# GpSimd takes 1536 of the 4096 columns in every round of an expert ranking's comparisons

## The reference

```python
logits = tokens @ router_w.T
probs = jax.nn.softmax(logits, axis=-1)
top1_idx = jnp.argmax(probs, axis=-1)
top1_prob = jnp.max(probs, axis=-1)
order = jnp.lexsort((-top1_prob, top1_idx))     # by expert, then most certain first, then by index
...
keep_sorted = pos_in_group < capacity           # ceil(4096 / 8 * 1.25) = 640
keep = jnp.zeros((T,), bool).at[order].set(keep_sorted)
return jnp.where(keep, top1_idx, 0).astype(jnp.int32)
```

## Time and profile before

| | |
|---|---|
| runs | 5526.91, 5540.9 and 5541.35 us, median 5540.9 |
| profiled execution | span 5525.2 us from the first to the last instruction; its own device time is not recorded apart from that |
| busy over the span | TensorE 4705.2 us (85%), VectorE 3719.1 (67%), ScalarE 2827.0 (51%), GpSimd 2810.2 (51%) |
| the 32 rounds | 3904.6 to 4002.9 us, 98.3 us or 1.8% of the span |

### The profile page before, as it was taken

The page is one execution under the profiler, slowest core; times in us unless marked ns, Lnnn a source line. Parts: engine busy times, 40 slices in busy tenths (PEclk is TensorE's granted clock), DMA queues, the critical chain, the costliest instruction groups (busy, mean ns, idle before and its releaser), DMA issues. The chain is left out here.

```text
span 5525.2 us, 143465 instructions
## 1 busy us (share of the span) xinstructions
PE 4705.2 (85%) x57069; PEld 3341.4 (60%) x57103; DVE 3719.1 (67%) x8589; ACT 2827.0 (51%) x6227; POOL 2810.2 (51%) x3349
## 2 busy tenths in 40 slices
PE   7699999999999999999999999954375999945886
PEld 3366666666666666666666666633263666623665
DVE  7677777777777777777777677748724656667442
ACT  2266565666666656666666656631022666641332
POOL 4477666777677667766777667601022333311000
PEclk9899999999999999999999999977587999967897
DMA  0211111111111111111111110000211000010002
GB/s 21 70 29 25 25 34 35 25 25 34 36 25 25 31 31 29 25 34 31 28 24 34 25 24 20 17 24 2 67 50 32 2 2 1 1 24 13 26 29 56
DMA packets 312162, 150.60 MB, mean 27 GB/s; under 512 B 146143, under 2 KB 301003, under 8 KB 311243
## 3 DMA queue, kind: packets, MB, share of 16 engines
q1 hardware_dynamic: 309451, 137.20, 10.3%
q0 software_dynamic: 2048, 4.20, 0.3%
HBM read 101.10 MB, written 27.41 MB: 23 GB/s over the span
## 5 line engine op out<-in xcount | busy, mean ns | idle before, releaser
L1435 POOL TENSOR_TENSOR loc_a<-loc_a,loc_b 128x512 f32<-128x512 f32 x768 | 976.9, 1274 | 234.0 <-DVE loc_b L1511 233.5
L1123 PE MATMUL psum<-loc_wqk,loc_xt 128*128 128x512 f32 x1536 | 828.9, 622 | 15.3 <-issue 4.7
L1186 PE MATMUL psum<-loc_m,xn_rows 128*128 128x128 f32 x6144 | 823.7, 277 | 4.8 <-DVE y_rows L1543 3.0
L1307 ACT ACTIVATE loc_sq<-psum 128x512 f32<-128x512 f32 x768 | 455.1, 593 | 682.6 <-PE psum L1123 681.3
L1460 POOL TENSOR_TENSOR loc_a<-loc_a,loc_rn 128x512 f32<-128x512 f32 x768 | 785.4, 1045 | 0.1
L1186 PEld LDWEIGHTS psum<-loc_m,xn_rows 128*128 128x128 f32 x6144 | 754.3, 193 | 48.2 <-issue 45.5
L1507 DVE TENSOR_TENSOR loc_a<-psum,loc_rope 128x512 f32<-128x512 f32 x768 | 523.2, 681 | 332.4 <-ACT loc_sq L1307 318.3
L1467 POOL TENSOR_TENSOR xn_cols<-xn_cols,loc_rec 128x512 f32<-128x512 f32 x384 | 394.1, 1047 | 685.3 <-DVE loc_rec L1538 684.9
L1344 ACT COPY xn_rows<-psum 128x512 f32<-128x512 f32 x768 | 411.7, 588 | 219.6 <-PE psum L1174 215.9
L1511 DVE TENSOR_TENSOR loc_b<-psum,loc_rope 128x512 f32<-128x512 f32 x768 | 520.5, 678 | 0.0
L1515 DVE TENSOR_REDUCE loc_n<-loc_sq 128x8 f32<-128x512 f32 x768 | 516.9, 673 | 0.0
(11 more groups left out here) (372 smaller groups left out, 8565.0 us busy)
## 6 DMA issues: line engine op xcount, KB each, us to landing
loc_x<-loc_shifted SPq DMA_DIRECT2D x192, 256.0 KB, 4.0
loc_shifted<-y_rows SPq DMA_DIRECT2D x144, 64.0 KB
loc_wqk<-in_L_ffn_Wqkv SPq DMA_DIRECT2D x24, 256.0 KB, 3.7
x_rows<-y_rows SPq DMA_DIRECT2D x96, 64.0 KB
x_rows<-y_rows SPq DMA_DIRECT2D x96, 63.5 KB
moe_w<-in_L_ffn_W SPq DMA_DIRECT2D x16, 256.0 KB, 4.7
l3a_qk<-l3a_rot SPq DMA_DIRECT2D x16, 256.0 KB, 2.1
grp_w<-in_L_ffn_W SPq DMA_DIRECT2D x16, 256.0 KB, 4.2
```

The source lines that it names most:

```text
L1123: nc.tensor.matmul(ring("p", i, unit), xt[:, b % 2, t * P:(t + 1) * P], wqk[:, unit * 512:(unit + 1) * 512], start=True, stop=True).then_i ...
L1186: last = nc.tensor.matmul(y_bank[:, 0:P], u[:, i % 2, h // 2, h % 2, :], m[:, h, :], start=(h == 0), stop=(h == HEADS - 1))
L1307: nc.scalar.activation(sq[:, g % 2, :], ring("p", i, unit), ACT.Square).then_inc(sem["squared"], 1)
L1435: nc.gpsimd.tensor_tensor(part, part, b_[:, g % 2, :], ALU.add).then_inc(sem["added"], 1)
```

## The change

In each round the 1536 columns that lie farthest from the diagonal block are compared by GpSimd: the last 1536 in rounds 0 to 15, the first 1536 in rounds 16 to 31. VectorE compares the other 2560, with as many instructions as before. TensorE waits in each round for both, VectorE's `compared` and the new `far_compared`. GpSimd waits, like VectorE, for `counted` before it writes a half of `above` again.

```diff
             names = ("turned", "router_ready", "logits_done", "exp_ready", "shifted", "top_ready", "top_stored", "top_spread",
-                     "onehot_ready", "compared", "counted", "blank_ready", "dve_step")
+                     "onehot_ready", "compared", "far_compared", "counted", "blank_ready", "dve_step")
...
+            FAR = 12 * P
+            early = lambda j: j < NT // 2
...
                         pe.wait_ge(sem["compared"], j + 1)
+                        pe.wait_ge(sem["far_compared"], j + 1)
...
                     nc.gpsimd.memset(core.y[:, :, :], 0.0).then_inc(sem["blank_ready"], 1)
+                    pool.wait_ge(sem["top_ready"], 1)
+                    pool.wait_ge(sem["top_spread"], 16)
+                    for j in range(NT):
+                        if j >= 2:
+                            pool.wait_ge(sem["counted"], j - 1)
+                        far = slice(TOK - FAR, TOK) if early(j) else slice(0, FAR)
+                        nc.gpsimd.tensor_scalar(above[:, j % 2, far], row[:, far], top[:, j:j + 1], None,
+                                                ALU.is_le if early(j) else ALU.is_lt).then_inc(sem["far_compared"], 1)
...
-                        after(nc.vector.tensor_scalar(above[:, m, 0:d1], row[:, 0:d1], mine, None, ALU.is_lt))
+                        start, stop = (0, TOK - FAR) if early(j) else (FAR, TOK)
+                        after(nc.vector.tensor_scalar(above[:, m, start:d1], row[:, start:d1], mine, None, ALU.is_lt))
...
-                            nc.vector.tensor_scalar(above[:, m, d1:TOK], row[:, d1:TOK], mine, None, ALU.is_le)
+                            nc.vector.tensor_scalar(above[:, m, d1:stop], row[:, d1:stop], mine, None, ALU.is_le)
```

## The result

| | before | after |
|---|---|---|
| time, median of 5 runs | 5532.54 us | 5621.43 us |
| runs from, to | 5526.91, 5541.35 | 5617.63, 5631.2 |
| ratio after / before | | 1.0165, 95% interval 1.0151 to 1.0179 |
| span of the profiled execution | 5525.2 us | 5618.9 us |

A forecast was written before the change was run, and what follows sets the result against it. VectorE's four instructions were taken to bound the 32 rounds; each loses 2.53 us to GpSimd and saves 0.80, so 1.73 us longer, 55.5 us in all, span 5580.7 us, median 5590 us, range 5543 to 5640.

The forecast's parts named there:

- the forecast's own band: For the 32 rounds: a loss of 1.9 to 3.2 us a round, +35 to +77 us, given 42%.
- the raw row: Rival, 18%: GpSimd's comparison really costs 2.58 ns per column and holds VectorE throughout; round 6.19 us, +101 us, about 5636 us.
- What bounds the rounds, and that a microsecond in a round is 32 in the end: In the 32 rounds VectorE's four instructions set the 3.03 us pace; nothing hides it, so 1 us a round makes 32 us.
- What VectorE gives up, 0.80 us a round: VectorE's comparisons lose 1536 columns at 0.519 ns each; alone its round falls from 3.03 to 2.23 us, saving 25.5 us.
- That the engines exclude each other: In the rounds GpSimd and VectorE take turns, so VectorE's round becomes 2.23 us plus the time GpSimd holds it up.
- The 2.53 us of GpSimd's hold: GpSimd's 1536-column comparison at 1.65 ns per column holds VectorE up 2.53 us in each round.
- the cleaning of the 512-column row: A GpSimd row outside the rounds: 1.633 us less 0.60 of supposed waiting and 0.19 fixed leaves 0.84 us, 1.65 ns per column.
- TensorE's second wait and GpSimd's wait for `counted` at nothing: In the rounds both waits add nothing, at most the end of one round; GpSimd may be a round ahead of VectorE.
- Line rate: Rival, 22%: GpSimd compares at its memset pace, 0.83 ns per column; a round loses 1.28 us, the kernel 15.5, about 5550 us.
- Beside each other: Rival, 12%: GpSimd's comparison holds VectorE up under 0.80 us a round or not at all; at best 25.5 us less, about 5515.
- Its tell-tales: Signs in the rounds: 32 GpSimd rows of 2.5 us or more, stretched VectorE rows summing to some 150 us, matmuls every 4.8 us.

The follow-up runs named there:

- the run beside: Kernel before, VectorE still comparing all 4096 columns; GpSimd adds the same 32 comparisons of 1536 columns into a tile nobody reads or waits for: 6.54 us a round.
- the probes: Kernel before, with single GpSimd instructions (512 to 1536 columns) ahead of the rounds, each beside 24 short VectorE instructions; 768 columns stretched one-input ones twice by 0.64 us.
- the run with three instructions: Changed kernel with GpSimd's 1536 columns a round split into three instructions of 512 columns in place of one: 5.79 us a round.

## Why the prediction was right, and where not

Measured 5621 us, predicted 5590, range 5543 to 5640, slower with 0.76. It is slower, by 1.6%. The cost of the change was put at 55.5 us and is 89 us. That lies above the forecast's own band (+35 to +77 us, 42%) and below the rival of the raw row (+101): none of the stated cases names it. The time is within the range because the range reaches up to that rival, not because the forecast's sum was right.

**What bounds the rounds, and that a microsecond in a round is 32 in the end: right.** 89.7 us in the rounds of one profile, 89 us between the medians. That they agree so closely is in part luck, since the rest of the kernel wanders by more than their difference. TensorE's granted clock stayed at 0.50, as it was forecast.

**What VectorE gives up, 0.80 us a round: right.** With ScalarE as the partner 1024 columns saved what the slope says (1024 x 0.519 = 0.53 us, 3.03 to 2.50). The 1536 columns were not measured without a hold; between the run beside and the changed kernel they are worth 6.54 - 5.85 = 0.69 us. The missing 0.11 us lie in the holds: in the run beside GpSimd meets `tie`, which costs VectorE less, 22 times instead of 14.

**That the engines exclude each other: right in direction, too simple in form.** Shown by GpSimd's work beside VectorE with nobody waiting for it: 3.51 us more a round. The prediction left open whether they take turns by whole instructions or by parts of one, and reckoned with the whole. The Trainium skill's page SBUF — State Buffer, section "Who interferes with whom", says that whoever comes first has the shared ports for its whole instruction. For GpSimd's two-input instructions and for its cast (1.46 us) I have seen nothing else. For its tensor-scalar instruction the probes contradict it: up to 1024 columns VectorE stands still twice for a third of the time, and between the two it is free. Here the measurement decides.

**The 2.53 us of GpSimd's hold: the term that was mis-sized.** The step that failed is the cleaning of the 512-column row: "So GpSimd seems to have waited 0.20 + 0.40 us and to have been ahead at the end." It had not waited to speak of: 512 columns take 1572 ns with nothing beside, against the row's 1633. That VectorE's `cd_u` and `cd_base` ran undisturbed inside it fits the probes: `cd_u` falls into the part that keeps nobody out, `cd_base` has two inputs, which the last part does not keep out, and the stretched one-input `cd_gap` at 4901.76 meets that last part. This is read off the sizes of the parts; that place itself was not tried again. The raw row gave 4.15 us for the instruction (0.19 + 3.96), and 4.16 us is what it takes.

Of this VectorE loses 3.51 us in the run beside (6.54 - 3.03), where the forecast had 2.53. So the sum should have been 32 x (3.51 - 0.80) = 87 us, and 89 are measured: nearer to the rival "the raw row" (+101) than to the forecast (+55.5). In the changed kernel the loss is 3.62 us by the pace (5.85 - 2.23) and 3.6 us by the count of held rows above. It is less than the 3.96 of the rival since it depends on what GpSimd meets: the probes are held for 3.90 us with one input (4.08 - 0.18) and for 3.02 with two (3.23 - 0.21), and half of the 32 holds in the rounds fall on instructions with two inputs.

**TensorE's second wait and GpSimd's wait for `counted` at nothing: right.** TensorE waits for VectorE alone in the profile after, and a third buffer changes nothing (5.88 against 5.85 us). GpSimd does wait for `counted`, 42.2 us in all, but nobody waits for it.

**The rivals.** Line rate falls: 2.52 ns per column where 0.83 was needed. The raw row had the price of the instruction right and the hold too long; it also called GpSimd the slower engine, and that is wrong, as its 4.15 us are less than a round of 6.19 or of 5.85, and TensorE waits for VectorE. The Trainium skill's sentence on one-input work (GPSIMD Engine Reference, "4.1 Engine selection") holds here for the cast (0.83 ns per column, as the memsets) and not for a comparison. "Beside each other" falls with the probes and the run beside. It would have needed a hold of 1536 columns under 0.80 us. Fewer columns do not help either: with 512 GpSimd holds VectorE for 0.42 us at a time, but saves it only 0.27 us a round, and there GpSimd is late.

**Its tell-tales.** GpSimd's rows of over 2.5 us and the stretched small instructions were seen as said. VectorE's sum was to be some 150 us and is 184.6, and the pace of 4.8 us was 5.85.

## What to carry to other kernels

Before work goes to an idle engine, ask whether that engine can work at the same time as the one it relieves: look in the trace for one instruction of each that overlap, and compare the row's maximum with its median. What the change takes off the busy engine (here 0.80 us a round) must be more than the time for which the helper keeps that engine standing (here 3.5 us). That the helper is idle and its own time free says nothing of this. An instruction that runs undisturbed inside another engine's long row does not show that the other one was waiting: it may have been in a part that shares nothing, and one measurement of that instruction alone would have shown its price. Here ScalarE took 1024 columns in two passes with a gain where GpSimd could not take them in one; the gain is 0.17% of the kernel.

## What the runs showed of the hardware that I had not expected

- GpSimd's tensor-scalar instruction costs 2.52 ns per column (1572 and 4157 ns for 512 and 1536), and hardly less with a constant or a float32 output (1490 and 4086); a cast costs 0.83 ns per column ((1464 - 611) / 1024) and a subtraction with a broadcast second input 1.67 ((2747 - 1042) / 1024).
- At 512, 768 and 1024 columns it keeps a one-input VectorE instruction out in two parts of about 0.83 ns per column with about as long a free part between, and a two-input one in the first part alone. From 1152 columns on VectorE stands still for 2.7 us and more in one stretch: with 1536 columns 3.02 us with two inputs and 3.90 with one.
- The exclusion works both ways: 512 columns take GpSimd 3.30 us beside VectorE's long comparisons and 1.57 alone, and in the run with three instructions 2.77 us beside them and 1.56 with VectorE idle. 768 columns take 3.60 us beside them; alone they would take 2.2, an estimate from 512 and 1536.
